# A gated graph network kernel: loads of the opening regrouped, and the first product ordered by chunks of the state

## What is computed

```python
h = x
for _ in range(T):
    a_in = einsum('nm,bmd->bnd', adj, h)
    a_out = einsum('nm,bmd->bnd', adj, h)
    av = concatenate([a_in, a_out], axis=-1)
    z = sigmoid(lin(av, w3, w3_b) + lin(h, u3, u3_b))
    r = sigmoid(lin(av, w4, w4_b) + lin(h, u3, u3_b))
    hv = tanh(lin(av, w5, w5_b) + lin(r * h, u5, u5_b))
    h = (1.0 - z) * h + z * hv
out = layernorm(x + h, axis=-1)
```

## Time and profile before

| | |
|---|---|
| median of 3 runs | 735.25 us (735.22 to 735.64) |
| profiled execution, its own time | 734.97 us |
| its span on the core | 732.9 us |
| TensorE matmul busy | 726.1 us (99%), 3237 instructions |
| TensorE weight load busy | 602.3 us (82%) |
| VectorE busy | 635.7 us (87%) |
| ScalarE busy | 419.4 us (57%) |
| GpSimd busy | 29.9 us (4%) |
| DMA | 124.13 MB, mean 169 GB/s |

### The profile page before, as it was taken

How to read it: one execution, slowest core, us unless ns; L and a number is a source line. 1 busy time by engine, 2 the same in 40 slices (tenths; PEclk the granted TensorE clock), 3 DMA queues, 4 the chain that set the end, 5 groups by cost and what they waited for, 6 DMA issues and landing times.

```text
span 732.9 us, 9687 instructions
## 1 busy us (share of the span) xinstructions
PE 726.1 (99%) x3237; PEld 602.3 (82%) x3237; DVE 635.7 (87%) x932; ACT 419.4 (57%) x647; POOL 29.9 (4%) x71
## 2 busy tenths in 40 slices
PE   9999999999999999999999999999999999999997
PEld 7888888888888888888888888888888888888886
DVE  6788898889998888898999888899899987899887
ACT  5645655465666654565566754565556664565546
POOL 0000000000010000000011000000011000000013
PEclk9999999999999999999999999999999999999999
DMA  8145454446766445445567445544467544544442
GB/s 345 61 145 168 136 184 143 140 148 186 237 225 194 160 148 172 152 137 167 188 237 229 156 139 172 184 140 134 163 203 254 195 159 143 164 132 134 142 145 116
DMA packets 74183, 124.13 MB, mean 169 GB/s; under 512 B 8368, under 2 KB 55472, under 8 KB 74160
## 3 DMA queue, kind: packets, MB, share of 16 engines
q1 hardware_dynamic: 72144, 116.43, 48.8%
q10 hardware_dynamic: 2016, 7.41, 2.8%
HBM read 67.18 MB, written 56.62 MB: 169 GB/s over the span
## 4 chain that ended last, share of the span: by engine, by line
PE 98%; DVE 1%; ACT 0%; issue 0%; POOLq 0%; POOL 0%; DVEq 0%
PE ps_g L420 17%; PE ps_g L418 17%; PE ps_g L419 17%; PE ps_v L420 12%; PE ps_v L418 12%; PE ps_v L419 12%; PE ps_a L420 3%; PE ps_a L418 3%; PE ps_a L419 3%; PE ps_g L510 1%; PE ps_a L438 1%; PE ps_g L549 0%; PE ps_v L510 0%; DVE dz L1072 0%; DVE stats L1037 0%
## 5 line engine op out<-in xcount | busy, mean ns | idle before, releaser
L685 ACT ACTIVATE ps_v<-ps_v,bias 128x512 f32<-128x512 f32 x94 | 62.2, 662 | 182.7 <-PE ps_v L420 182.7
L418 PE MATMUL ps_g<-aT_hi,wt_lo 128*128 128x512 f32 (+1 forms) x380 | 147.1, 387 | 0.0
L420 PE MATMUL ps_g<-aT_hi,wt_hi 128*128 128x512 f32 (+1 forms) x380 | 147.0, 387 | 0.0
L419 PE MATMUL ps_g<-aT_lo,wt_hi 128*128 128x512 f32 (+1 forms) x380 | 147.0, 387 | 0.0
L724 ACT ACTIVATE z<-ps_g,bias 128x512 f32<-128x512 f32 x94 | 64.8, 690 | 95.0 <-PE ps_g L420 94.6
L418 PEld LDWEIGHTS ps_g<-aT_hi,wt_lo 128*128 128x128 f32 x380 | 71.3, 188 | 14.6
L419 PEld LDWEIGHTS ps_g<-aT_lo,wt_hi 128*128 128x128 f32 x380 | 71.3, 188 | 14.5
L420 PEld LDWEIGHTS ps_g<-aT_hi,wt_hi 128*128 128x128 f32 x380 | 71.3, 188 | 14.5
L870 DVE TENSOR_TENSOR aT_lo<-aT,aT_hi 128x1024 fp32r<-128x1024 f32 x46 | 56.4, 1225 | 30.4 <-ACT aT_hi L660 30.4
L860 DVE STREAM_TRANSPOSE ab<-ps_a 128x1024 f32<-128x1024 f32 x46 | 57.4, 1249 | 23.5 <-PE ps_a L420 22.3
L418 PE MATMUL ps_v<-rh_hi,wt_lo 128*128 128x512 f32 x192 | 74.7, 389 | 0.0
(11 more groups left out here) (126 smaller groups left out, 1237.0 us busy)
## 6 DMA issues: line engine op xcount, KB each, us to landing
turned_a<-ab SPq DMA_DIRECT2D x46, 512.0 KB, 3.7
aT<-turned_a SPq DMA_DIRECT2D x184, 128.0 KB, 3.0
turned_h<-hb SPq DMA_DIRECT2D x46, 512.0 KB, 2.6
hn<-turned_h SPq DMA_DIRECT2D x184, 128.0 KB, 3.0
x_in<-in_x_rows SPq DMA_DIRECT2D x14, 512.0 KB, 4.6
xT<-in_x_cols SPq DMA_DIRECT2D x12, 512.0 KB, 4.3
out<-y ACTq DMA_DIRECT2D x12, 512.0 KB, 3.6
wide<-in_w_t SPq DMA_DIRECT2D x3, 512.0 KB, 6.6
```

Of the source, the lines that this page charges most:

```text
L418: nc.tensor.matmul(dst, lhs_lo, rhs_hi, start=first, stop=False, skip_group_check=True)
L419: nc.tensor.matmul(dst, lhs_hi, rhs_lo, start=False, stop=False, skip_group_check=True)
L420: return nc.tensor.matmul(dst, lhs_hi, rhs_hi, start=False, stop=last, skip_group_check=True)
L685: nc.scalar.activation(ps_v[:, oc, :], ps_v[:, oc, :], ACT.Tanh, bias=bias[:, BV, oc:oc + 1]).then_inc(v_ready, 1)
```

## The change

The rows of the first group come in two loads: two graphs with the adjacency (320 KB) into `first_in`, the other two (256 KB) straight into `y[0]`, which is free then. Both are issued by ScalarE, and `lead` after them. SP waits for a new semaphore, `lead_issued`, instead of `neg_half_ready`; its first load is chunk 1 of the state together with W4, side by side in DRAM (768 KB), its second W5 with the biases; W3 and the rest follow as before. TensorE does 11 transposes instead of 13, waits for the second half of the rows before the second half of the aggregate, and goes through U3 chunk by chunk, low part of the state included. ScalarE makes the high part of state chunk 1 after the two halves of the aggregate; VectorE adds the biases after the sum of W5.

```diff
-        wide = [sb(f"wide{k}", [P, 2, C, D]) for k in range(3)]
-        lead_in = sb("lead_in", [P, C * D + C * ROWS])
+        lead_in = sb("lead_in", [P, C * D + C * ROWS + 2 * C * D])
+        w5_in = sb("w5_in", [P, 2 * C * D + 5 * C])
+        wide = [sb("wide0", [P, 2, C, D])]
+        wide += [t.rearrange("p (h c d) -> p h c d", h=2, c=C)
+                 for t in (lead_in[:, C * D + C * ROWS:], w5_in[:, 0:2 * C * D])]
...
-        first_in = sb("first_in", [P, GB * D + N])
-        adjT = first_in[:, GB * D:GB * D + N]
+        first_in = sb("first_in", [P, HB * D + N])
+        adjT = first_in[:, HB * D:HB * D + N]
...
-        x_first = [first_in[:, 0:GB * D].rearrange("p (b d) -> p b d", b=GB), y[1]]
+
+        def x_first(j, b, cols):
+            if j == 0 and b < HB:
+                return first_in[:, b * D + cols.start:b * D + cols.stop]
+            return y[j][:, b, cols]
...
-        xT_first = [lead_loaded, sem("xT_first1")]
+        xT_first = [lead_loaded, w_loaded[W4]]
...
-            sp.wait_ge(neg_half_ready, 1)
-            sp.dma_start(xT[0][:, 1, :], x_cols[0, :, 1, :]).then_inc(xT_first[1], DMA)
-            load_wide(W4)
-            sp.dma_start(bias_in[:, :, :], biases).then_inc(bias_loaded, DMA)
-            load_wide(W5)
-            load_wide(W3)
-            sp.dma_start(x_first[1][:, :, :], second_rows).then_inc(rows_second, DMA)
+            sp.wait_ge(lead_issued, 1)
+            sp.dma_start(lead_in[:, C * D + ROWS:], second_lead).then_inc(w_loaded[W4], DMA)
+            sp.dma_start(w5_in[:, :], w5_b).then_inc(w_loaded[W5], DMA)
+            sp.dma_start(wide[W3][:, :, :, :], w3_t).then_inc(w_loaded[W3], DMA)
+            sp.dma_start(y[1][:, :, :], second_rows).then_inc(rows_second, DMA)
...
             def first_aggregate(j):
 
-                pe.wait_ge(rows_second if j == 1 else rows_first, DMA)
                 for hf in range(2):
+                    if j == 0:
+                        pe.wait_ge((rows_first, rows_rest)[hf], DMA)
+                    elif hf == 0:
+                        pe.wait_ge(rows_second, DMA)
...
                     pe.wait_ge(u3_lo_ready, 1)
                     for oc in range(C):
                         part(ps_g[0], wt_lo, U3, oc, kc, hT_hi, False, False)
-                for kc in range(C):
                     pe.wait_ge(hT_lo_ready, kc + 1)
                     for oc in range(C):
                         part(ps_g[0], wt_hi, U3, oc, kc, hT_lo, False, False)
...
                 pe.wait_ge(ident_ready, 1)
-                keep_warm(13)
+                keep_warm(11)
                 first_aggregate(0)
...
             act.dma_start(first_in[:, :], first_rows).then_inc(rows_first, DMA)
+            act.dma_start(y[0][:, HB:GB, :], first_rest).then_inc(rows_rest, DMA)
             act.dma_start(lead_in[:, 0:C * D + ROWS], lead).then_inc(lead_loaded, DMA)
+            act.sem_inc(lead_issued, 1)
 
             act.wait_ge(neg_half_ready, 1)
             nc.scalar.activation(table_probe[:, :], neg_half[:, :], ACT.Sigmoid)
-            for c in range(C):
-                h_high(0, 0, c, first=True)
+            h_high(0, 0, 0, first=True)
             for hf in range(2):
                 first_a_high(0, hf)
+            h_high(0, 0, 1, first=True)
             weight_high(W4)
...
             weight_low(W4)
-            dve.wait_ge(bias_loaded, DMA)
+            sum_halves(W5)
+            dve.wait_ge(w_loaded[W5], DMA)
             for b, (l, r) in ((BZ, (0, 1)), (BR, (2, 1)), (BV, (3, 4))):
                 nc.vector.tensor_tensor(bias[:, b, :], bias_in[:, l, :], bias_in[:, r, :],
                                         ALU.add).then_inc(bias_ready, 1)
-            sum_halves(W5)
             sum_halves(W3)
```

More of the change, by code:

```diff
@@ L56, with build @@
 EPS = 1e-5
-def build(nc, x_rows, first_rows, second_rows, lead, x_cols, w3_t, w4_t, w5_t, u5_t, biases, out_rows):
+def build(nc, x_rows, first_rows, first_rest, second_rows, lead, second_lead, x_cols, w3_t, w5_b, u5_t, out_rows):
     N, B, D = out_rows.shape
@@ L97, in build @@
         table_probe = sb("table_probe", [P, GB])
-        bias_in = sb("bias_in", [P, 5, C])
+        bias_in = w5_in[:, 2 * C * D:].rearrange("p (l c) -> p l c", l=5)
         bias = sb("bias", [P, 3, C])
@@ L101, in build @@
         wt_lo = [sb(f"wt_lo{k}", [P, C, D], F32R) for k in range(5)]
-        first_in = sb("first_in", [P, GB * D + N])
-        adjT = first_in[:, GB * D:GB * D + N]
+        first_in = sb("first_in", [P, HB * D + N])
+        adjT = first_in[:, HB * D:HB * D + N]
         W3, W4, W5, U3, U5 = range(5)
         BZ, BR, BV = range(3)
-        xT = [lead_in[:, C * D:].rearrange("p (c r) -> p c r", c=C)]
+        xT = [lead_in[:, C * D:C * D + C * ROWS].rearrange("p (c r) -> p c r", c=C)]
         xT += [sb(f"xT{q}", [P, C, ROWS]) for q in range(1, SLOTS)]
@@ L175, in build @@
         w_loaded = [sem(f"w_loaded{k}") for k in range(5)]
-        lead_loaded, bias_loaded = sem("lead_loaded"), sem("bias_loaded")
+        lead_loaded = sem("lead_loaded")
         ident_zero, ident_ready, neg_half_ready = sem("ident_zero"), sem("ident_ready"), sem("neg_half_ready")
@@ L183, in build @@
         x_loaded = [sem(f"x_loaded{k}") for k in range(2)]
-        rows_first = sem("rows_first")
+        rows_first, rows_rest = sem("rows_first"), sem("rows_rest")
+        lead_issued = sem("lead_issued")
         stored = [sem(f"stored{k}") for k in range(2)]
         xT_loaded = [sem(f"xT_loaded{q}") for q in range(SLOTS)]
-        xT_first = [lead_loaded, sem("xT_first1")]
+        xT_first = [lead_loaded, w_loaded[W4]]
         xh_ready = [sem(f"xh_ready{q}") for q in range(SLOTS)]
@@ L369, in _ @@
                 sp.sem_inc(stored[k], DMA)
-            wide_in = [w3_t, w4_t, w5_t]
-            def load_wide(k):
-                sp.dma_start(wide[k][:, :, :, :], wide_in[k]).then_inc(w_loaded[k], DMA)
-            sp.wait_ge(neg_half_ready, 1)
-            sp.dma_start(xT[0][:, 1, :], x_cols[0, :, 1, :]).then_inc(xT_first[1], DMA)
-            load_wide(W4)
-            sp.dma_start(bias_in[:, :, :], biases).then_inc(bias_loaded, DMA)
-            load_wide(W5)
-            load_wide(W3)
-            sp.dma_start(x_first[1][:, :, :], second_rows).then_inc(rows_second, DMA)
+            sp.wait_ge(lead_issued, 1)
[3 more added lines that the diff above has]
+            sp.dma_start(y[1][:, :, :], second_rows).then_inc(rows_second, DMA)
             load_cols(0, 1)
@@ L438, in first_aggregate @@
                             done = nc.tensor.matmul(bank[:, c, bb * N:(bb + 1) * N],
-                                                    x_first[j][:, b, c * P:(c + 1) * P],
+                                                    x_first(j, b, slice(c * P, (c + 1) * P)),
                                                     adjT[:, :], start=True, stop=True)
@@ L1181 @@
         "x_rows": x.reshape(B // GB, GB, N, C, QUADS, BLK).transpose(0, 2, 4, 3, 1, 5).reshape(B // GB, N, GB * D),
-        "first_rows": np.concatenate([x[0:GB].transpose(1, 0, 2).reshape(N, GB * D), adj.T], axis=1),
+        "first_rows": np.concatenate([x[0:GB // 2].transpose(1, 0, 2).reshape(N, GB * D // 2), adj.T], axis=1),
+        "first_rest": x[GB // 2:GB].transpose(1, 0, 2),
         "second_rows": x[GB:2 * GB].transpose(1, 0, 2),
@@ L1185 @@
                                 x[0:GB].reshape(GB * N, C, P)[:, 0, :].T], axis=1),
+        "second_lead": np.concatenate([x[0:GB].reshape(GB * N, C, P)[:, 1, :].T,
+                                       features_first(w("w4"), 2).reshape(P, 2 * C * D)], axis=1),
         "x_cols": x.reshape(B // GB, GB * N, C, P).transpose(0, 3, 2, 1),
         "w3_t": features_first(w("w3"), 2),
-        "w4_t": features_first(w("w4"), 2),
-        "w5_t": features_first(w("w5"), 2),
+        "w5_b": np.concatenate([features_first(w("w5"), 2).reshape(P, 2 * C * D),
+                                np.stack([np.asarray(inputs[f"L0_gnn_{k}_b"]).reshape(C, P) for k in bias_names])
+                                .transpose(2, 0, 1).reshape(P, len(bias_names) * C)], axis=1),
         "u5_t": features_first(w("u5"), 1)[:, 0],
-        "biases": np.stack([np.asarray(inputs[f"L0_gnn_{k}_b"]).reshape(C, P) for k in bias_names]).transpose(2, 0, 1),
     }
```

## The result

The changed kernel took **740.41 us** (median of 14 runs, 736.45 to 742.49) against 735.25 (735.12 to 735.75, 14 runs): slower by 5.2 in the median and by 0.6% in the mean (ratio 1.0058, 95% interval 1.0045 to 1.0071). The forecast was 735.35, no difference to be told, with a range to 736.1. Not one of the 14 runs lies in it. As telling as the median is the spread: 0.6 us before, 6 us after.

A forecast was written before the change was run, and what follows sets the result against it. TensorE, busy 99% of the span, was taken as the bound, so only its opening mattered. W4 beginning 0.2 later less 0.1 for W5's wait gave +0.1 us on 735.25: 735.35 us, range 734.8 to 736.1.

The forecast's parts named there:

- The new wait for chunk 1: In the product with U3, TensorE waits 0.4 us for chunk 1's high part, whose load lands with W4 at 7.8.
- the head start: The aggregate starts at 3.95 instead of 4.55 and ends near 6.6 instead of 7.08, a lead of 0.45 us.
- W5's wait: In the product with W5, the 0.09 us wait for ScalarE's high part of W5 goes.
- W3's cover: Before W3, both halves of r are ready at 14.90 and W3 begins at 15.39; the 0.4 us cover holds.
- all the change can give or take lies where TensorE is not yet in its loop: Loops are untouched, so only the opening matters; W3's shift passes to the end one for one.
- 11 transposes: In the opening, the useless transposes end at 3.93, so the aggregate can start at about 3.95.
- A difference that arises behind 20 us: A listed sign that the forecast is wrong: time gained or lost later than 20 us into the run.
- a landing is set by the bytes ahead of it: In the opening, loads are served in issue order with full DMA engines: lead at 5.86, chunk 1 with W4 at 7.8.
- Rival A: Chunk 1 with W4 lands by 7.3, so U3 runs without a gap: gain 0.4, 734.9 us; chance 0.20.
- costs nothing: SP's first load, issued at about 2.1 instead of 1.55, loses nothing since its data are served only from 4.5.
- Rival B: SP's load takes turns with ScalarE's, the lead lands near 7.0 to 7.8, W4 about 1.0 later: 736.3; chance 0.05.
- Rival C: TensorE's clock rises late, between the eleventh transpose and first aggregate, slowing aggregate and U3: +3, 738.3; chance 0.02.

The follow-up runs named there:

- b_warm11_pad: The kernel before with 11 transposes instead of 13 and four idle TensorE instructions in their place: median 735.47 us.
- after_again: The changed kernel run again, unaltered, for its spread and a second trace: 736.97, 737.75, 742.57 us (lowest, median, highest of 10 runs).
- one_rows: The changed kernel with the first rows in one load of 576 KB again: median 737.15 us, none of 8 runs above 738.
- b_order: The kernel before with only U3 taken chunk by chunk, no load moved: median 735.33 us.
- b_warm11: The kernel before with 11 transposes instead of 13 and nothing else: median 737.10 us.
- rest_only: The changed kernel with the first rows in one load and chunk 1 and W4 in separate loads: median 737.09 us.
- rest_pad: rest_only with four idle instructions at the start of TensorE's code: median 735.64 us.
- after_pad: The changed kernel with four idle instructions at the start of TensorE's code: median 736.90 us, 2 of 7 runs above 738.
- pad_rows: The changed kernel with the rows of SP's first load 8192 bytes apart in DRAM instead of 6144, same bytes moved: median 739.91 us.
- split_pad: The changed kernel with chunk 1 and W4 in separate loads and four idle TensorE instructions: median 736.69 us, 1 of 11 runs above 738.
- hold_sp: The changed kernel with SP waiting until the lead has landed before issuing its first load: median 741.22 us.
- hold_warm: hold_sp with 20 more transposes on TensorE ahead of its wait for chunk 1: median 740.05 us.
- one_pad: The changed kernel with the first rows in one load and four idle TensorE instructions: median 736.03 us, none of 11 runs above 738.
- lead_two: rest_pad with the lead in two loads, U3 and chunk 0 of the state: median 736.16 us, no run above 738.
- after: The first profiled execution of the changed kernel, compared with the kernel before: 740.52 us.

## Why the prediction was wrong

**The right parts.** First rows at 3.9 and the aggregate at 3.96 (forecast 3.95), over by 6.4 (6.6). The new wait for chunk 1 is there and uses up the head start, W5's wait is gone, the order by chunks is free, W3's cover holds.

**Step that failed, first: "all the change can give or take lies where TensorE is not yet in its loop".** It lay also where TensorE leaves it. "11 transposes" was costed for the opening alone, where it is 0.25 us by b_warm11_pad; as a program of another length it cost 1.3 to 1.9 us at 713 us in seven of the nine traces of kernels that had it without the idle instructions. The changed kernel's own first trace is not among the seven: there all 5.4 us lie in the opening, so a run at 740.5 needs none of it. "A difference that arises behind 20 us" was among the signs of being wrong, and it came. No rival held this.

**Second, and the larger: "a landing is set by the bytes ahead of it".** That holds for the order of the loads, and for the mean engine. A load lands with its slowest engine, and the trace of one execution had shown a good one. Now single rows took 0.4 to 1.8 us instead of 0.08 to 0.23. Two terms of the sum rest on it. The lead was to land 0.1 late, at 5.86; it landed at 9.77, and in after_again at 5.8. SP's load was put at 7.8, with 8.3 as the far end; it landed at 8.9 in after_again, and in the seven traces of kernels that merge it and do not hold it back between 7.9 (one_rows) and 10.0. So the wait for chunk 1 was 1.14 and not 0.4. Rival A, an earlier landing, falls with it. In b_order and b_warm11, with all loads as before, the lead landed at 6.2 and 6.1 where it was 5.8: even the kernel before has less room than its one trace lets one think.

One term that was put at nothing was not tried alone: that SP waits for `lead_issued` "costs nothing". In the four traces with SP's loads as before (before, b_order, b_warm11, b_warm11_pad) chunk 1 landed at 6.4 to 6.9 and W4 at 7.7 to 8.2. In rest_only and rest_pad, with the same bytes ahead, it was 7.0 and 7.2, and 8.4 and 8.5. They issue the first load 0.14 later and read from other arrays; which of the two it is, no run tells. In rest_pad TensorE then waits for the low part of chunk 1, which VectorE makes behind W4's sum.

**Rival B** (queues share the engines) had 0.05 and was argued away by the earlier trace rows. These show the order across queues while all engines keep step. An engine that lagged behind had both queues' rows before it and went by turns, 0.39 us apart; by the estimate above that made a delay of 1.3 us into 3.9. The Trainium skill (DMA: Bandwidth & Descriptors, Queues, rings and completion order) says that each engine goes round among the queues it has work for; the trace agrees for that engine. The rival's price was +1.0; the opening cost 5.4 in that trace. **Rival C** had the right resource and for the most part the wrong place. The clock rose between 4.5 and 7.2 us in every trace, and a late rise did cost: most of the 0.5 us of one_rows. What cost more was that it fell later in three traces, after an idle time of 2.2 to 4.1 us. C was priced at +3 and given 0.02; with B it forms one chain: late row, shared engine, idle TensorE, lower clock. It should have been one rival with one chance.

**The sum of 5.2 us** (740.41 - 735.25) is not one price: it is the median of executions with different histories. In those without a long delay the opening costs 1.3 to 1.4 (after_again, after_pad) and the code 1.3: 737.5 to 737.9, as six of ten runs in after_again. Three runs at 736.5 in the first batch are lower than that by about the code's 1.3; no trace shows them. In traces with a long delay the opening costs 2.8 (pad_rows), 3.6 (split_pad) and 5.4. Of the 24 executions of the changed kernel 14 lay above 738, 11 of 14 in the first batch and 3 of 10 in the second. What makes it vary so is open; the batches ran on several chips, and the chip was not tried alone. Open too is what holds up a single row for over 1 us, and why this comes with the rows in two loads (30 of 73 executions of kernels with them lay above 738, hold_sp and hold_warm left out, and 1 of 80 of those with one load): neither 6 KB rows (pad_rows, one_pad) nor a third load (lead_two) brought it. That the first rows' second half is written to another tile, or read from another array, was not tried alone. Nor is it settled why the traced executions with a delay of over 5 us in the opening (the changed kernel's first, hold_sp's) have no gap at 713 us, with the same code.

No version beat the kernel before. b_order (735.33) and b_warm11_pad (735.47) equal it within what can be told.

## What to carry to other kernels

An edit to an engine's code moves all the code behind it. After a loop, the next block may come late, and an "issue" gap of 1 to 2 us there can be code, not data, as it was here. Before and after a change of the number of instructions, look at the first straight stretch behind a loop, and try a few idle instructions at the start. When a load gates the critical engine, count its slowest engine over several executions, hold other queues' loads back only if they can afford the delay, and do not split it for a head start of half a microsecond.

## What the runs showed of the hardware

- A row of 4 KB that takes 0.16 us in most cases took 1.47 (the changed kernel), 1.25 and 1.56 (split_pad); two of 2 KB took 1.8 instead of 0.08 (split_pad). In the changed kernel one such row decided when the whole load landed.
- Where one engine had rows of two queues before it, they came by turns, row by row: 0.16 + 0.23 = 0.39 us apart in the changed kernel and pad_rows, 0.16 + 0.08 = 0.24 in split_pad, whose other load has rows of 2 KB. Engines that kept step finished the earlier load first: SP's load, issued at 1.55, moved nothing until 4.5 us in the kernel before.
- Idle times of TensorE of 4.1, 2.5 and 2.2 us (after, hold_sp, split_pad) were each followed by 3.4 us at the lower level of the clock, beginning 0.1 to 1.5 us after work had resumed; one of 3.4 us in pad_rows and one of 1.1 in after_again were not. In hold_warm, with 20 transposes in the idle time, it did not fall.
- Code came in blocks of 16 KB on q8: none between 302 us and 709, while TensorE's loop went round. The first block behind it came 4 us ahead of its use, or, where the gap was, 2.3 to 2.7 us before the product that had to stand for it.
